# Who subtracts the rounded probabilities: VectorE in place of GpSimd, in an fp32 cross-attention

## The reference

```
a = layer_norm(ctx) * gamma + beta
Q = x @ Wq.T;  K = a @ Wk.T;  V = a @ Wv.T          # split into 16 heads of 64
attn = softmax(Q @ K.T * 64 ** -0.5)                # over 64 keys
out = (attn @ V) merged over heads @ Wo.T
return x + tanh(gate) * out
```

## Time and profile before

| | |
|---|---|
| median of 3 runs | 1524.88 us |
| the profiled execution, its own time | 1520.95 us |
| its span | 1519.2 us |
| TensorE busy | 1478.4 us (97%), 6624 matmuls |
| VectorE busy | 1146.3 us (75%) |
| ScalarE busy | 893.7 us (59%) |
| GpSimd busy | 525.2 us (35%) |
| GpSimd's remainders (L650) | 112 of 1456 ns mean, 163.0 us |
| DMA | 348.52 MB, mean 229 GB/s |

### The profile page before, as it was taken

How to read it: one execution, slowest core, us unless ns; L and a number is a source line. 1 busy time by engine, 2 the same in 40 slices (tenths; PEclk the granted TensorE clock), 3 DMA queues, 4 the chain that set the end, 5 groups by cost and what they waited for, 6 DMA issues and landing times.

```text
span 1519.2 us, 20234 instructions
## 1 busy us (share of the span) xinstructions
PE 1478.4 (97%) x6624; PEld 1194.7 (79%) x6624; DVE 1146.3 (75%) x1349; ACT 893.7 (59%) x1894; POOL 525.2 (35%) x364
## 2 busy tenths in 40 slices
PE   6999999999999999999999999999999999999999
PEld 5666788788888788888787788877778787787887
DVE  6345788687878787878866787878878787777843
ACT  4456645454545455546675776766667666666721
POOL 5334000000000000000123675666766566766741
PEclk9999999999999999999999999999999999999999
DMA  7699865566565656565489887777887887888842
GB/s 272 208 384 390 295 219 182 200 208 214 193 215 191 218 180 229 180 208 175 145 270 337 259 254 237 239 226 230 241 258 238 228 248 212 238 250 244 246 145 72
DMA packets 305736, 348.52 MB, mean 229 GB/s; under 512 B 37216, under 2 KB 178656, under 8 KB 305632
## 3 DMA queue, kind: packets, MB, share of 16 engines
q1 hardware_dynamic: 305632, 347.23, 71.7%
HBM read 198.26 MB, written 145.75 MB: 226 GB/s over the span
## 4 chain that ended last, share of the span: by engine, by line
PE 57%; DMA 12%; SPq 10%; issue 7%; DVE 6%; POOL 5%; ACT 4%; DVEq 0%; ACTq 0%; POOLq 0%
PE banks L1169 18%; PE banks L1170 17%; PE banks L1171 17%; DMA p_by_key<-p_scratch 4%; SPq L469 4%; PE banks L1198 3%; POOL p_parts L650 3%; DMA out<-c_out 3%; SPq L489 2%; DMA probs<-s_scratch 2%; DVE a_ring L955 2%; ACT probs L799 2%; POOL probs L644 1%; DVE parts L961 1%; DMA wo_split_scratch<-wo_ring 1%
## 5 line engine op out<-in xcount | busy, mean ns | idle before, releaser
L1169 PE MATMUL banks<-parts,a_ring 128*128 128x512 f32 x1792 | 701.7, 392 | 12.0 <-DVE a_ring L955 11.3
L1171 PE MATMUL banks<-parts,a_ring 128*128 128x512 f32 x1792 | 698.1, 390 | 0.0
L1170 PE MATMUL banks<-parts,a_ring 128*128 128x512 f32 x1792 | 698.0, 390 | 0.0
L1169 PEld LDWEIGHTS banks<-parts,a_ring 128*128 128x128 f32 x1792 | 336.7, 188 | 89.1 <-DVE a_ring L955 18.3
L1171 PEld LDWEIGHTS banks<-parts,a_ring 128*128 128x128 f32 x1792 | 336.7, 188 | 70.9
L1170 PEld LDWEIGHTS banks<-parts,a_ring 128*128 128x128 f32 x1792 | 336.9, 188 | 68.9
L799 ACT ACTIVATE probs<-probs,neg_max 128x64 f32<-128x64 f32 x1024 | 258.7, 337 | 1.7 <-DVE neg_max L1061 1.7
L1047 DVE TENSOR_TENSOR c_out<-banks,c_out 128x1024 f32<-128x1024 f32 x159 | 192.7, 1212 | 85.7 <-PE banks L1171 59.5
L650 POOL TENSOR_TENSOR p_parts<-p_by_key,p_parts 128x512 fp32r<-128x512 f32 x112 | 163.0, 1456 | 213.2 <-ACT p_parts L808 213.0
L955 DVE TENSOR_TENSOR a_ring<-a_sum,a_ring 128x1024 fp32r<-128x1024 f32 x128 | 185.6, 1450 | 66.7 <-ACT a_ring L735 66.3
L735 ACT CAST a_ring<-a_sum 128x1024 fp32r<-128x1024 f32 x128 | 134.3, 1050 | 164.8 <-PE banks L1171 132.7
(11 more groups left out here) (76 smaller groups left out, 1309.6 us busy)
## 6 DMA issues: line engine op xcount, KB each, us to landing
xq<-x_t SPq DMA_DIRECT2D x32, 1024.0 KB, 6.5
s_scratch<-c_out SPq DMA_DIRECT2D x64, 512.0 KB, 3.1
probs<-s_scratch SPq DMA_DIRECT2D x128, 256.0 KB, 3.8
c_out<-x SPq DMA_DIRECT2D x64, 512.0 KB, 5.0
out<-c_out SPq DMA_DIRECT2D x63, 512.0 KB, 4.7
b_raw<-m_scratch SPq DMA_DIRECT2D x29, 1024.0 KB, 6.7
m_scratch<-m_stage SPq DMA_DIRECT2D x16, 1792.0 KB, 13.9
p_scratch<-p_turned SPq DMA_DIRECT2D x448, 64.0 KB, 2.6
```

What stands on the lines that cost most here:

```text
L1169: pe.matmul(to, wl, mh, start=first, stop=False, skip_group_check=joined)
L1170: pe.matmul(to, wh, ml, start=False, stop=False, skip_group_check=joined)
L1171: return pe.matmul(to, wh, mh, start=False, stop=last, skip_group_check=joined)
```

## The change

The remainders of units 16 to 127 (`p_by_key - high part`, 128 x 512, both inputs in SBUF) are issued by VectorE, by the `split_p_lo` that it had for the first 16 units, in that place of its order. GpSimd's `split_p_lo` is gone. All waits and counts of the other engines are the same.

```diff
@@ -643,13 +643,6 @@
-            def split_p_lo(u):
-                pool.wait_ge(p_hi_made, u + 1)
-                if u == ON_PE:
-                    pool.wait_ge(p_lo_made, ON_PE)
-                nc.gpsimd.tensor_tensor(p_parts[:, u % 2, 1, :], by_key(u), p_parts[:, u % 2, 0, :].bitcast(F32),
-                                        ALU.subtract).then_inc(p_lo_made, 1)
-
@@ -660,9 +653,6 @@
                 for z in (2 * s, 2 * s + 1):
-                    for u in units(split_slot, z):
-                        if u >= ON_PE:
-                            split_p_lo(u)
                     for u in units(soft_slot, z - SUM):
                         normalise(u)
@@ -1080,7 +1070,7 @@
             def split_p_lo(u):
                 dve.wait_ge(p_hi_made, u + 1)
-                nc.vector.tensor_tensor(p_parts[:, u % 2, 1, :], banks[:, 6, :], p_parts[:, u % 2, 0, :].bitcast(F32),
+                nc.vector.tensor_tensor(p_parts[:, u % 2, 1, :], by_key(u), p_parts[:, u % 2, 0, :].bitcast(F32),
                                         ALU.subtract).then_inc(p_lo_made, 1)
@@ -1143,8 +1133,7 @@
                     for u in units(split_slot, z):
-                        if u < ON_PE:
-                            split_p_lo(u)
+                        split_p_lo(u)
                     for u in units(soft_slot, z - TURN):
```

## The result

Ten runs of each kernel gave 1532.17 us for the changed kernel (median, 1528.11 to 1536.81) and 1523.88 us for the kernel before (1516.83 to 1528.76). The ratio is 1.0056, 95% interval 1.0037 to 1.0075: slower by half a per cent, 8.3 us. The forecast was 1529.7 us, 4.8 us more than before.

The account below looks back on a forecast made before the run. TensorE's queue was taken to set the time. The terms, +8.3 us for delayed `turn_blocks`, -3.5 us for port relief and the rest 0, gave +4.8 us: 1529.7 us against the 1524.88 us median, range 1516 to 1546.

Parts of the forecast that it names:

- the case to which I gave 0.38: Slower than the forecast by more than 0.5%: the first rival (0.24) and the second rival (0.14) taken together.
- the second rival: `turn_blocks` pushed back, no relief on the port VectorE and GpSimd share: +8.3 to +15 us, middle 1536.5 us; chance 0.14.
- What bounds the kernel: TensorE's queue, busy 97% of the span, sets the time; only its gaps can be won or widened.
- Part 1: GpSimd loses 112 remainders, 163.0 us of its time; it has idle time, so this is worth nothing.
- Part 2: VectorE gains 112 remainders at 0.69 us each, 77 us, which fit in its 152 us of idle time: 0.
- Part 3: Remainder ahead of `turn_blocks` delays SP's stores and fetches, then ACT and TensorE, 0.69 us in 12 rounds: +8.3 us.
- Part 4: VectorE would wait for ACT's rounding ahead of 24 remainders, 20.1 us in all; counted 0, up to +20 us uncovered.
- Part 5: Port shared by VectorE and GpSimd: `sum_a` runs sooner and blocks fewer `a_ring` subtractions; -3.5 us, bounds 0 and -7.1.
- Part 6: Remainder ready sooner or later for products with V and fetches: shifts cancel, 0; bounds 0 and -6.8 us.
- The first rival: VectorE falls behind as remainders wait for `normalise`; `turn_blocks` and `split_a_lo` come late: +21.6 us, 1546.5 us; chance 0.24.
- The third: Rival: SP's other waits absorb the shift, `a_ring` gaps and fetch waits shrink: -9.4 us, 1515.5 us; chance 0.12.

## Why the prediction was right, and where it was not

The time, 1532.17 us, lies in the range and 2.5 us above the forecast, and the sign was right. The loss itself was 8.3 us where I had added up 4.8 us; the time came nearer than that because the ten runs of the kernel before had a median 1.0 us under the one that I started from. The ratio of 1.0056 is just over the 0.5% that I had called the same, so what came is the case to which I gave 0.38. In its terms it is the second rival: a push and no relief, at the lower end of its +8.3 to +15 us, but with part of the loss from late remainders, which the second rival did not count.

*What bounds the kernel.* Right: the ratios mostly follow TensorE's gaps in the table.

*Part 1, GpSimd's time is worth nothing.* Right: it is busy 285.56 us in the stage in place of 432.07, and waited 379.5 us for VectorE's reciprocals.

*Part 2, 0.69 us each, hidden.* The price was mis-sized: 1.10 us, 123.1 us in place of 77. That it was hidden is not shown for the remainders themselves. A row sum behind `turn_blocks` put 57 us more on VectorE than before and cost nothing, but with `turn_blocks` first the remainders still cost 0.34%.

*Part 3, +8.3 us by the push.* The mechanism is shown. A push of 0.67 us alone, without the change, cost 0.64%, 9.7 us of 1519.92, and nothing when it stood behind. For the changed kernel the term is too large: the gaps that end with ACT's emptying grew by 5.4 us in the profiled execution, and taking the remainder from ahead of `turn_blocks` gave back 0.29%, some 4.4 us. The sign that I had written down for this part failed too: the unnamed gaps were to go up to some 26 us, and the part was to be wrong if they stayed. They stayed, at 17.8 us. They were a poor measure, since the waits that are named after the emptying rose (5.0 to 9.4 us) and so did the gaps taken from the starts; what carries the part is the pair with the row sum.

*Part 4, VectorE waits for ACT's rounding, 20.1 us in 24 places, counted at 0.* Measured 22.9 us in 18. Whether it costs was not tried by itself.

*Part 5, -3.5 us of relief.* This step failed. VectorE got back 30 us on the `a_ring` subtractions, but the gaps ahead of steps only went from 5.7 to 5.3 us (4.1 without the slower matmuls). Cutting `sum_a` to nearly nothing took 3.8 us of those gaps away and did not change the time of the kernel before. With `turn_blocks` first the relief was gone from the changed kernel (1.79 and 1.82 us a subtraction), and it was faster all the same. I take it that TensorE loses at the next late fetch what it gains ahead of a step; no run shows where the gain went.

*Part 6, the remainder's lateness, 0.* Failed by 3.6 us in the profiled execution: three products with V waited for it. (The three began 0.05 us after their remainders ended.) I had put the remainder's lock against `normalise`, and that came for 53 of them, at 1.16 us; the long ones are against `sum_a`, which had moved forward with the remainder gone from GpSimd. VectorE's and GpSimd's timelines of the changed kernel at one of them, and PE's:

```profile
1143.97 0.69 DVE L1051 TENSOR_REDUCE neg_max<-probs 128x8 f32<-128x512 f32 x1 [0.75 <-DMA probs<-s_scratch]
1144.57 2.66 DVE L1073 TENSOR_TENSOR p_parts<-p_by_key,p_parts 128x512 fp32r<-128x512 f32 x1
1147.15 0.70 DVE L1068 STREAM_TRANSPOSE p_turned<-probs 128x512 f32<-128x512 f32 x1
...
1143.30 1.04 POOL L644 TENSOR_TENSOR probs<-probs,row_rec 128x512 f32<-128x512 f32 x1 [2.79 <-DVE row_rec L1060]
1144.30 2.38 POOL L638 TENSOR_TENSOR a_sum<-xq 128x1024 f32<-128x1024 f32 x1
...
1147.28 0.50 PE L1158 MATMUL banks<-p_parts,v_diag 128*128 128x512 f32 x1 [1.59 <-DVE p_parts L1073]
```

`sum_a` began 0.27 us ahead, the remainder took 2.66 us, the product with V started as it ended, and `turn_blocks` stood behind it too. This is the rule of the Trainium skill, "SBUF — State Buffer", "Who interferes with whom", in one picture: with two SBUF inputs on VectorE and a GpSimd instruction that reads SBUF, the second to start waits out the first. The trace agrees: 2.38 - 0.27 + 0.69 = 2.80 us, measured 2.66.

*The first rival* (VectorE falls behind, +21.6 us) had its condition nearly met, remainder and wait together 1.30 us of the 1.36 us of idle time. Its consequence did not come in that size. The 30 us that the `a_ring` subtractions gave back were not in that count; that they are the reason was not tried. *The third* had its reliefs in part (the fetches' waits for a remainder went from 6.8 to 4.3 us), but nothing took the shift up, as it needed.

## What to carry to other kernels

When an in-order engine feeds a DMA queue that is mostly busy, look first not at how full the engine is but at what stands ahead of the one instruction that the queue waits for: here 0.67 us placed ahead of it in 112 places cost 0.64%, the same work behind it nothing. Before moving work between engines, look for the instruction that others hang on and move that one forward; here it gave 0.45% with no work removed. A gap of TensorE taken away at the place where it shows is no gain until the time is seen to fall: with ACT's emptying first it came back ahead of another operand, and with the sums cut down the time did not move.

## What the runs showed of the hardware

Two things I had not expected. The first is how much of VectorE's time the locks took. In the kernel before, 48 of the 108 `a_ring` subtractions from 800 to 1490 us began while GpSimd was idle and took 1.22 us in the mean, and 44 began during `sum_a` and took 2.30 us. In the changed kernel 31 of 105 began during `sum_a`, at 1.95 us, and the others took 1.21 us: some 30 us less, of which 25 us are fewer and shorter locks by `sum_a`, an instruction that the change had only moved.

The second is what a gap of TensorE can cost besides itself. In the 14 traces, from 170 us on and but for the last 10 us, the granted clock fell to 0.50 in 28 stretches, 27 of 3.4 us and one of 6.8. Each began when TensorE was standing idle or had begun again less than 1.5 us before, behind a gap of 1.9 to 3.5 us (distance of starts less 0.227 us). Not every such gap had one behind it: one of 3.5 us in the kernel before with `turn_blocks` first had none. A stretch of 3.4 us holds 5 to 8 matmuls at 0.43 us from start to start in place of 0.23 and costs 1.3 to 1.7 us. The ten runs of the changed kernel have a mean granted clock of 0.996, those of the kernel before beside the experiments 0.998. An estimate from the two is 1 to 2 stretches more in a run, some 2 of the 8.3 us. The push does not need it: the row sum ahead of `turn_blocks` cost 0.64% at a mean clock of 0.998.
